# Attention step of an adaLN block with a routed feed-forward part: query and key halves in turn, normalised rows and three causal masks on GpSimd

## The reference

```python
h = _layernorm(x, axis=-1) * (1 + ca) + sa
x = x + ga * _L0_attn_ref(h, wq, wk, wv, wo)
h = _layernorm(x, axis=-1) * (1 + cb) + sb
x = x + gb * _L0_ffn_ref(h, Wr, br, W1, b1, W2, b2)
...
# attention
q = _rope(_rmsnorm(jnp.einsum('bim,mhd->bhid', x, wq)))
k = _rope(_rmsnorm(jnp.einsum('bim,mhd->bhid', x, wk)))
v = jnp.einsum('bim,mhd->bhid', x, wv)
s = jnp.einsum('bhid,bhjd->bhij', q * mult, k * mult)
s = s - 1e30 * mask          # mask: key after query
o = jnp.einsum('bhij,bhjd->bhid', jax.nn.softmax(s, axis=-1), v)
return jnp.einsum('bhid,hdm->bim', o, wo)
```

## Time and profile before

| | us |
|---|---|
| median of 3 runs (1123.93 to 1126.92) | 1124.4 |
| the profiled execution, time | 1132.29 |
| the profiled execution, span of the records | 1130.5 |
| TensorE busy in the span | 1018.9 |
| ScalarE busy | 963.0 |
| VectorE busy | 896.2 |
| GpSimd busy | 785.7 |

### The profile page before, as it was taken

One profiled execution on the slowest core, in us unless ns is written; L12 is line 12 of the kernel. 1 busy time (PEld: TensorE's weight loads), 2 busy tenths in 40 slices (PEclk: granted clock), 3 DMA queues, 4 the chain that ended last, 5 costly groups with the idle time before them and its releaser, 6 DMA issues. The chain is left out here.

```text
span 1130.5 us, 27394 instructions
## 1 busy us (share of the span) xinstructions
PE 1018.9 (90%) x7294; PEld 780.5 (69%) x7294; DVE 896.2 (79%) x2757; ACT 963.0 (85%) x3517; POOL 785.7 (70%) x1197
## 2 busy tenths in 40 slices
PE   5899999999999999999999999999898779989700
PEld 3588888888888888888888888888554434558600
DVE  5788888889998889888888888886768746767647
ACT  6999999999999999999999999997797748888424
POOL 6655578877787877777777777777356675656654
PEclk9999999999999999999999999999999988999955
DMA  5410000100000100000000000000442322320158
GB/s 151 132 34 13 14 17 26 37 25 23 24 23 27 35 15 13 16 16 15 16 16 16 14 16 15 16 15 18 126 112 92 97 77 65 90 68 26 37 188 271
DMA packets 53849, 57.91 MB, mean 51 GB/s; under 512 B 8108, under 2 KB 42783, under 8 KB 53700
## 3 DMA queue, kind: packets, MB, share of 16 engines
q1 hardware_dynamic: 36612, 35.11, 10.5%
q0 software_dynamic: 8640, 16.87, 4.5%
q10 hardware_dynamic: 8448, 4.20, 1.3%
HBM read 33.08 MB, written 23.97 MB: 50 GB/s over the span
## 5 line engine op out<-in xcount | busy, mean ns | idle before, releaser
L753 ACT ACTIVATE squares<-unit 128x128 f32<-128x128 f32 x1024 | 273.3, 303 | 3.6 <-PE unit L1225 3.4
L565 POOL TENSOR_TENSOR roped<-roped,rope_b 128x512 f32<-128x512 f32 x132 | 175.1, 1327 | 91.7 <-DVE rope_b L1085 89.3
L753 ACT ACTIVATION_READ_ACCUMULATOR squares<-unit 128x1 f32 x1024 | 235.2, 236 | 0.0
L1567 POOL DMA_INDIRECT y_rows<-y_out,place_y x142 | 152.2, 1072 | 94.7 <-DVE y_out L1989 49.4
L1085 DVE TENSOR_TENSOR rope_b<-unit,sin_sb 128x512 f32<-128x512 f32 x256 | 174.4, 681 | 14.6 <-ACT squares L753 12.3
L731 ACT ACTIVATE probs<-scores,rr 128x256 f32<-128x256 f32 x256 | 124.3, 485 | 43.5 <-issue 27.4
L1046 DVE SCALAR_TENSOR_TENSOR acc<-pv,den,acc 128x128 f32<-128x128 f32 x448 | 146.2, 341 | 0.3
L1312 PEld LDWEIGHTS unit<-ident_wr,roped 128*128 128x128 f32 x1024 | 117.9, 141 | 31.6 <-ACT k_t L770 13.0
L1312 PE MATMUL unit<-ident_wr,roped 128*128 128x128 f32 x1024 | 135.2, 275 | 1.6 <-POOL roped L565 1.5
L1975 DVE TENSOR_TENSOR hid_lo<-hidden,hid_hi 128x512 f16<-128x512 f32 (+1 forms) x144 | 92.3, 685 | 54.1 <-ACT hid_hi L1675 34.5
L574 POOL TENSOR_TENSOR roped<-roped,rr 128x1024 f32<-128x1024 f32 x64 | 121.5, 1899 | 13.0 <-DVE roped L1120 12.2
(11 more groups left out here) (304 smaller groups left out, 3061.3 us busy)
## 6 DMA issues: line engine op xcount, KB each, us to landing
shared<-y_rows SPq DMA_DIRECT2D x16, 512.0 KB, 5.6
x_all<-in_L_attn_x SPq DMA_DIRECT2D x32, 128.0 KB, 2.2
h_late<-in_L_ffn_W SPq DMA_DIRECT2D x16, 256.0 KB
out_x<-hidden ACTq DMA_DIRECT2D x16, 256.0 KB, 3.4
rope_b<-x_rows SPq DMA_DIRECT2D x13, 258.0 KB
tile_x<-x_rows SPq DMA_DIRECT2D x12, 258.0 KB
y_rows<-y_out,place_y POOLq DMA_INDIRECT x142
ga_b<-mod_dram SPq DMA_DIRECT2D x32, 64.0 KB
```

The costliest lines, as they stand in the source:

```text
L565: pool.tensor_tensor(out=roped[parity][:, u, heads], in0=roped[parity][:, u, heads], in1=rope_b[:, u % 2, heads], op=ALU.add)\
L753: nc.scalar.activation(squares[:, c * D:(c + 1) * D], UN[0][:, c * D:(c + 1) * D], ACT.Square, accum_out=ssq[parity][:, u * H + c:u * H + ...
L1567: pool.indirect_dma_start(out=y_rows, out_offset=bass.IndirectOffsetOnAxis(ap=place_y[i % (2 * SLOTS)][:, s:s + 1], axis=0), in_=y_out[at] ...
```

## The change

The projections come in another order: half h // 2 % 2 of the queries (even h) and of the keys (odd h) in turn, first for token tile 0 (h = 0 to 3), then for tile 1 (h = 4 to 7). So the in-place slots of VectorE, those with three operations, are now 0, 2, 4 and 6, and `add` on GpSimd is called for h = 1, 3, 5 and 7. The normalised rows `xn` and `xn2` are made by GpSimd (`normal_rows`, four 128x128 instructions) instead of ScalarE, and the offsets go. For heads 4, 5 and 6 the mask product on TensorE goes, and the first two score products become one of 256 columns; instead GpSimd sets the masked parts of the exponentials to zero (`zero_ahead`, 128x256), and PV of these heads waits for it. The list of GpSimd in a step is written in another order.

```diff
-    NCH = NLN + 4 * TT
+    NCH = NLN + 2 * TT
...
+        ZEROED = (4, 5, 6)
+
+        def projection(h):
+
+            kind, half, t = h % 2, h // 2 % 2, h // HH
+            return kind, half, t, kind * TT + t
...
-                    wait(pool, "xn_ready", cap(TT * n, TT * NB))
-                    wait(pool, "xn2_done", TT * (n - 5))
...
-                def offsets():
...
+                def normal_rows(k):
+
+                    b = (n + 1, n - 4)[k]
                     wait(pool, "rr_done", n + 2)
...
+                    wait(pool, ("tx_done", "h2t_done")[k], b)
+                    stats, dst = ((mv[other], xn), (mv2[parity], xn2))[k]
+                    for t in range(TT):
+                        c = NLN + k * TT + t
+                        pool.tensor_scalar(dst[:, t, :], x_all[:, TT * b + t, :], stats[:, t, 0:1], rr[other][:, c:c + 1],
+                                           ALU.subtract, ALU.mult).then_inc(S[("xn_ready", "xn2_done")[k]], 1)
...
+                def zero_ahead(h):
+
+                    wait(pool, "exp_done", 2 * (H * (n - 2) + h + 1))
+                    blocks = probs[:, h % NPR, :].rearrange("p (a c) -> p a c", c=P)[:, 0:TT + 1:TT, :]
+                    pool.affine_select(out=blocks, in_=blocks, compare_op=ALU.is_ge, fill=0.0, base=0,
+                                       pattern=[[0, TT], [1, P]], channel_multiplier=-1).then_inc(S["masked"], 1)
...
                     newton()
-                    offsets()
-                if n == 0:
-                    for h in range(1, HH):
-                        add(h)
+                if X:
+                    normal_rows(0)
+                if N2:
+                    normal_rows(1)
+                if A:
+                    add(1)
                 if rest:
                     scatter(n - 7, other, 1, 1)
                 if B:
...
+                if A:
+                    add(3)
                 if B:
-                    if A:
-                        wait(pool, "q_added", HH * n + 3)
                     scale_queries(1)
-                if now:
-                    scatter(n - 6, parity, 0, 0)
                 if X:
...
+                if C:
+                    zero_ahead(4)
+                if now:
+                    scatter(n - 6, parity, 0, 0)
...
+                if C:
+                    zero_ahead(5)
                 if A:
-                    add(4)
+                    add(5)
...
-                if A:
-                    add(5)
+                if C:
+                    zero_ahead(6)
...
-                    if X and h == (XN_AT if n else XN_AT + 1):
...
-                    if N2 and h == XN2_AT:
...
-                    in_place = h < HH and n > 0
+                    w = 2 * NU * n + h
+                    bank, half_of, t, u = projection(h)
+                    product = UN[0][:, bank * HH * D:(bank + 1) * HH * D]
+                    heads = slice(half_of * HH * D, (half_of + 1) * HH * D)
+                    in_place = h % 2 == 0
...
                     wait(pe, "exp_done", 2 * (g + 1))
+                    if h in ZEROED:
+                        wait(pe, "masked", len(ZEROED) * b + ZEROED.index(h) + 1)
...
+                        if h in ZEROED:
+                            nc.tensor.matmul(s[:, 0:T], k[:, h, 0:P], q[:, h, 0:T], start=True, stop=True)
+                            nc.tensor.matmul(s[:, T:T + P], k[:, h, P:T], q[:, h, P:T], start=True, stop=True)\
+                                .then_inc(S["s_done"], 1)
...
+                        if kind:
+                            wait(pe, "rope_done", w - 1)
+                        else:
+                            wait(pe, "q_added", w // 2)
```

119 lines of the change are left out of this document (41 added, 78 removed).

## The result

| | before | after |
|---|---|---|
| median, runs beside each other on one chip (us) | 1125.66 | 1310.91 |
| span of the profiled execution (us) | 1130.5 | 1310.7 |
| mean of a full step, steps 7 to 29 (us) | 24.15 | 30.76 |

The changed kernel is slower by the factor 1.1655 (1.1599 to 1.1711): 185 us more, where 112 were predicted and the range ended at 146. The direction was right, and so were the places of two of the three waits; the size was not. The ratios here are of executions in the faster of the chip's two states, and one of the four of e2, 1555 us long at a clock of 0.65, is not among them. Steps are counted from the transposes of `xn` in slot 4 to those of the next step.

What follows compares the result with a forecast made beforehand. TensorE was taken to bound the step, and to wait for GpSimd's late masks: 97.7 us over 24 full steps plus 6.4, 3.1, 2.9 and 2 make 112, so the median goes from 1124.4 to 1236 us, range 1216 to 1270.

Steps and rivals of the forecast that it cites:

- the range: Forecast bounds on the changed kernel's median, 1216 to 1270 us, from row and mask prices, other steps and the clock; about 85%.
- What bounds the kernel: Attention step of 24.15 us: TensorE bounds it, so its work taken away is worth its time and new waits cost fully.
- The mask products: TensorE, heads 4 to 6: three products of 0.11 us saved, 0.33 per step, 10.6 us over 32 steps.
- ScalarE: ScalarE loses four 128x128 instructions, 0.87 us per pair; not the bound, so worth nothing.
- The order of the projections: VectorE: one operation more in slots 4 and 6, one less in 1 and 3; costed only as a rival.
- VectorE alone: Rival: masks in time, but PV(7) waits for VectorE's sum of head 5; step up to 0.9 us longer, 1152 us; chance 4%.
- 28.2: Forecast length in us of a full attention step of the changed kernel, in place of 24.15, 4.07 more.
- the walk: GpSimd's list timed item by item to the masks: TensorE waits about 2.7 us ahead of PV(4), 1.4 ahead of PV(6).
- The price of a row: GpSimd, one 128x128 normalised row: taken as 0.30 us, between 0.24 and 0.46; four in series 1.20.
- The mask: GpSimd, one 128x256 mask: taken as 0.42 us, between 0.29 and 0.62; 0.40 by the skill's per-element figure.
- The light steps: Attention steps outside 7 to 30: 6.4 us for steps 2 to 5, 3.1 for 6, 2.9 for 31, 2 for 32 and 33.
- The clock: Rival: TensorE's clock falls to half in the gap ahead of PV(4), up to 1.0 us per step, +26, 1262 us; chance 12%.

Runs made afterwards that it cites:

- e2: The changed kernel with all masks back on TensorE, rows still on GpSimd, both new orders kept; ratio 1.1042 to the kernel before, mean step 28.79 us.
- e6: The kernel before with only the masks of heads 4, 5 and 6 moved to GpSimd; ratio 1.0029, mean step 24.28 us.
- e11: The kernel before with only VectorE's routing step `one_hot` moved from ahead of the sums of head 5 to behind them; ratio 0.9969, step 24.00 us.
- e10: e6 with `one_hot` on VectorE moved behind the sums of head 5; ratio 0.9922 to the kernel before, step 23.81, later 23.70 us.
- e9: The changed kernel with all its instructions, rows and masks at other places in GpSimd's list; ratio 1.0586 to the kernel before, mean step 26.16 us.
- e8: e1 with the masks of heads 4 and 6 moved ahead of add(3) and add(5) in GpSimd's list; ratio 1.0483, mean step 25.98 us.
- e3: The changed kernel with rows back on ScalarE and masks on TensorE, leaving both new orders; ratio 1.0463 to the kernel before, mean step 25.96 us.
- e1: The changed kernel with the normalised rows back on ScalarE, masks and orders as changed; ratio 1.091 to the kernel before, mean step 27.62 us.
- e7: The kernel before with 21 extra GpSimd instructions at its start, three each of seven forms, to price them; the row's form took 0.80 us.
- e4: The changed kernel with 13 extra unused TensorE products per step inside its waits, to hold the clock; ratio 1.1514 to the kernel before, step 30.36 us.

## Why the prediction was wrong, by its own steps

**What bounds the kernel** was right for the kernel before and too simple for what follows. "TensorE work taken away is worth its time" failed: e6 has three products less in a step and is no faster. In the earlier trace rows the scores of the next step come 1.49 after PV(6) starts at 622.44, where PV(6) and PV(7) need 0.67 each: 0.15 is a wait that I passed over. VectorE was as close behind as that, and e11, which takes `one_hot` away from ahead of the sum, gains just these 0.15.

**The mask products**: 0.33 per step. e10 against e11 gives 0.2 to 0.3 (24.00 less 23.81 and 23.70), once VectorE is out of the way. In the changed kernel it is nothing, since the chain sets the step.

**ScalarE**: worth nothing. Its busy time falls and nothing comes of it: e9, with the rows off ScalarE, is no faster than e8, which has them there. No run takes them off alone.

**The order of the projections**: put at nothing with the masks late; alone (with GpSimd's new list) it is 1.8 (e3, 1.6 in the later rhythm), where the rival, VectorE alone, gave up to 0.9. It is not to be added to the 28.2, since the walk goes through VectorE's slots 3 and 5. e1 bears that out: the walk without its rows and with the offsets, 28.2 less 1.20 and 0.34 more, gives 27.3, and e1 takes 27.5.

**The price of a row** is the term that was mis-sized. I took 0.30, "nearest to the 0.29 row" of an affine select, with 0.46 as the upper end; it is 0.79. Four rows in series are 1.96 longer than walked. 28.2 and 1.96 make 30.16, and the step without clock losses is 30.36. In 24 steps that term alone is 47 of the 61 us by which the full steps were short (24 times 30.76 less 28.2); the clock is 10 of the rest. The upper end came from ScalarE's pair, which says nothing about GpSimd; half of its 0.87 is 0.435, not 0.46, and no row shown gives 0.24 as the price of a row. GpSimd's own rows would have been a fairer end: its two-input operation on 128x256 takes 0.62, and a row with two operations and two more operands could have been as much or more. With 0.62 as the upper end the range would have reached 1287 (0.16 more for each of four rows in 26 steps, on 1270), still short. The Trainium skill (GPSIMD Engine Reference, section 4.1 Engine selection) says that one-input work is roughly at line rate there. The 0.41 of the mask agrees with the prediction's estimate of 0.40. The row doesn't: it takes 0.79, and in e7 128 more columns add 0.42 to its form, where the estimate had 0.11 for them. The measurement decides: this form is slower than a `tensor_tensor` of the same size.

**The mask**: 0.42 taken, 0.41 measured.

**The walk** was right in order and in each duration but one. It gave waits of 2.7 ahead of PV(4) and 1.4 ahead of PV(6), with 1.2 of rows in the first; in e1, which has no rows on GpSimd, they are 2.00 and 1.37. (The 2.7 were 3.1 less 0.4 by which a product ends after its successor could start; by the earlier trace rows that is 0.16, 617.60 and 0.39 less 617.83.) Its wait for `place_k` in slot 3 is there (2.87). It overlooked that projection 5 hangs on that slot too: by 28.2 it would have been hidden ahead of PV(4), and in the changed kernel a part of the wait only moves there (2.19 ahead of projection 5, 1.35 ahead of PV(4)). So it did not change the sum, but that is luck: the walk never looked at it.

**The light steps** were put at 14.4; the span gives 180.2 in all, less 24 times 6.61, that is 21.5. The part up to the transposes of step 7 is 18.8 longer, where the prediction had 9.5 for it; the part from step 31 to the last PV is 7.0 longer, where it had 4.9, and what follows the last PV is 4.3 shorter, for which I have no reason. Their rows cost more as well; how much of the 18.8 is theirs was not measured.

**The clock** was a rival with 12%, at 26 us. The mechanism came: 0.73 from 602 to 604 and 0.50 from 604 to 608, half of full speed, behind TensorE's wait of 2.19 that ends at 602.60. It came behind a wait at another place than the rival had it, ahead of projection 5 and not of PV(4). Its price by e4 is 16 us, of which the full steps show 10. The Trainium skill (TensorE: Matmul & The Clock Gate, Part 1: The HAM clock gate) says that the clock is throttled after idleness, and this trace agrees.

**The range** failed with it: it held the row's price at 0.24 to 0.46 and nothing of the clock on top of it. Both ends were from engines or operations other than the one in question, and the two unfavourable cases, price and clock, came together.

## What to carry to other kernels

Price an instruction on GpSimd by its own form: where the trace of before has none, keep the upper end at a multiple of the nearest form, not at another engine's time. When work is put on an in-order engine, ask what stands behind it and who waits for that: here the four rows and three masks cost 4.4 us in a full step at one place (or 4.8 with the clock) and 0.2 at another. And an engine that shows as the bound may have another 0.15 us behind it, so work taken from the first is worth its time only up to there.
